# Attention scores on 32 of TensorE's rows, maxima of two batches beside the experts, exponentials of two banks, in a layer of attention and experts

## The chip, the cores and the metric

The kernel runs on one core of a Trainium2 chip. The metric is device time in microseconds (us): the time of one execution. All times below are in us unless they are marked ns. TensorE does matmuls and transposes, VectorE (DVE) and ScalarE (ACT) work on elements and can read the matmul results in PSUM, GpSimd (POOL) works on SBUF and issues the gathers, SyncE (SP) issues the other DMAs. PSUM has eight banks of 512 float32 a partition.

## The reference

With x of 4 x 512 tokens of 512 features, the layer gives x + attention(xn) + experts(xn), with xn the layer norm of x. Attention has 8 heads of 8 features, for each of 4 batches of 512 tokens. The experts: each token takes the two best of 8 experts, and the mean of their rectified outputs.

```python
    scores = jnp.einsum('bhqd,bhkd->bhqk', q, k)
    attn = jax.nn.softmax(scores, axis=-1) / jnp.asarray(HEAD_DIM ** 0.5, x.dtype)
    out = jnp.einsum('bhsl,bhlv->bhsv', attn, v)
...
    logits = x @ W_gate + b_gate
    _, top_idx = jax.lax.top_k(logits, TOP_K)
    y_all = jax.nn.relu(jnp.einsum('bsd,edh->bseh', x, W_e) + b_e)
    y = jnp.take_along_axis(y_all, top_idx[..., None], axis=2)
    return y.mean(axis=2)
```

## The kernel before

The program has no scheduler: each engine's list of work is written out by hand, each engine runs its list in order, and semaphores tie the lists together. A number in parentheses is a line of the kernel.

**Stages.** First come layer norm, projections and routing (to about 107 us). Then 39 expert tiles of 128 gathered token rows (NS is 39). For each tile TensorE turns the next tile's rows with four transposes (1060) and runs twelve matmuls of 512 columns into ps_s (1080); ScalarE copies the turned rows (568) and does the ReLU (573); VectorE makes the low part (798) and adds the expert's bias (830); GpSimd adds half the output bias (475) and gathers later rows (460). Then comes attention: 32 units, eight a batch. A unit is one half of the heads (g, four heads) and 128 keys.

**A head on the array.** The queries and keys of four heads lie in one tile of 128 partitions, 32 a head (q_t, k_t): low and high parts, and in the first rows the negative row maximum against ones, so that a logit comes out of the matmul with its maximum already subtracted. k_head holds, for each head, a copy of the 32 rows of k_t with zeros in the other 96. A matmul over all 128 partitions thus gives one head. The copies are made by DMAs from SyncE (load_heads, 358); k_head is cleared by VectorE (835, 848) and GpSimd (473, 488, 490).

**Scores and maxima.** For the row maxima, scores (988) gives 128 queries against 512 keys of one head, into one bank, and maximum (803) reduces it on VectorE. A batch has 32 of each. The 32 of batch 0 run beside expert tiles, two a tile from tile 21 (SCORES_AT); the other 96 run in the attention units, four a unit, in the first 24 units (unit_scores, with LAG). lay_max (811) writes the finished maxima into the token-wise tile lay, and a fill turns them into q_t.

**Units.** logits (1004) gives 128 keys against 512 queries of one head in ps_t, which has two banks used in turn; ScalarE takes the exponential of one bank (629); values (1015) multiplies the four heads' exponentials with v and ones, 9 columns a head, in ps_o. TensorE's order in a unit is: two logits with a score behind each, the fills of the middle, the values of the unit before, two logits with scores, the fills of the end.

**Fills.** misc_plan (231) names the jobs between: k and q (turning a tile of keys or queries, 972), max, o (976), turn (980), out (984, 985: the output projection, which VectorE adds to the residual, 891). All go through ps_m, whose two banks are used in turn; a fill waits until its bank was read two jobs before. tile_jobs (245) names the fills beside expert tiles.

**Layout and sums.** lay_out (286) splits queries or keys into high and low parts in the tile lay, in one piece for each 128 tokens: by GpSimd for batches 0 and 3, by VectorE for 1 (in expert tiles 33 to 36) and 2 (after the experts). After the experts GpSimd gathers the experts' rows onto the residual in acc, 32 gathers (501), and the layout of q for batch 3 stands at i == 8 among them.

## Time and profile before

| | us |
|---|---|
| runs | 389.19, 388.20, 389.71 |
| median | 389.19 |
| span of the profiled execution | 390.1 |
| TensorE, matmuls, busy | 334.0 (86%) |
| VectorE busy | 260.2 (67%) |
| GpSimd busy | 204.8 (53%) |
| ScalarE busy | 172.6 (44%) |
| mean granted clock of TensorE, as a share of 2.4 GHz | 0.874 |

The profiled execution's own time is the span from its first to its last instruction, 390.1, 0.9 above the median of the runs. Busy TensorE time counts matmuls whose records overlap (a 512-column matmul has a record of 0.39 and starts 0.23 behind the one ahead), so it is read by starts, not by sums. A share of busy time is a mean over stages with different limits; the rows below are therefore taken by stage. "issue" as a releaser is time in which the engine waited for nothing that the profile shows. x8 in a row is eight records; the four values matmuls of a unit are eight records.

### The profile page before, as it was taken

The page shows a single profiled execution, that of the slowest core. Times are in us where ns is not written, and L with a number is a line of the kernel's source. Part 1 is how long each engine was busy: PE and PEld are TensorE (multiplying, and loading weights), DVE is VectorE, ACT ScalarE, POOL GpSimd, SP SyncE. Part 2 cuts the span into 40 slices and gives each one's busy share as a digit, 9 for nine tenths or more (in the row PEclk, how much of TensorE's full clock was granted, in tenths as well). Part 3 has the DMA queues.
Part 4 walks back from the last instruction along what each step waited for, and adds up shares of the span by engine and source line. Part 5 has one row for each costly group of instructions (what it writes and reads, how often), then busy time and mean ns, then how long its engine had stood idle before and what let it go on. Part 6 is the DMA issues. An engine that isn't in the chain of part 4 may idle for free.

```text
span 390.1 us, 5604 instructions
## 1 busy us (share of the span) xinstructions
PE 334.0 (86%) x1629; PEld 238.5 (61%) x1629; DVE 260.2 (67%) x583; ACT 172.6 (44%) x304; POOL 204.8 (53%) x216
## 2 busy tenths in 40 slices
PE   1386888684869999999999998939999999999965
PEld 1265777683848888888888876705455655544412
DVE  4288888857913444466767789597878889785313
ACT  1454444461023333333323322435786777667740
POOL 2155555556474777777665573276688888100000
PEclk9996555556559999999999999977999999999995
DMA  8776765315052545555544441254999999610112
GB/s 232 273 287 221 242 226 188 109 55 216 0 163 83 167 163 164 168 165 186 189 140 146 147 124 54 74 146 97 199 293 241 200 204 148 130 55 0 55 54 108
DMA packets 31004, 59.60 MB, mean 153 GB/s; under 512 B 5504, under 2 KB 5632, under 8 KB 30848
## 3 DMA queue, kind: packets, MB, share of 16 engines
q1 hardware_dynamic: 23248, 40.63, 29.9%
q0 software_dynamic: 7728, 18.62, 22.7%
q8 instruction: 15, 0.25, 0.3%
q14 instruction: 13, 0.11, 0.1%
HBM read 38.52 MB, written 18.61 MB: 146 GB/s over the span
## 4 chain that ended last, share of the span: by engine, by line
PE 67%; DVE 17%; issue 5%; ACT 5%; DMA 3%; SPq 2%; POOL 0%; ACTq 0%; DVEq 0%; POOLq 0%
PE ps_s L1080 28%; PE ps_t L1012 10%; PE ps_o L1027 8%; PE ps_s L1001 6%; PE ps_t L1060 4%; DVE small L678 3%; PE ps_m L972 2%; DVE t_lo L689 2%; DMA stage<-in_L_ffn_W_e_dram 2%; ACT probs L629 2%; DVE stats L661 2%; PE ps_s L946 2%; DVE small L669 2%; DVE hot_row L783 1%; PE ps_m L984 1%
## 5 line engine op out<-in xcount | busy, mean ns | idle before, releaser
L1080 PE MATMUL ps_s<-w_split,t_hi 128*128 x312 | 101.7, 407 | 2.2 <-issue 2.2
L629 ACT ACTIVATE probs<-ps_t 128x512 f32<-128x512 f32 x128 | 69.6, 597 | 34.7 <-PE ps_t L1012 26.7
L809 DVE TENSOR_REDUCE row_max<-ps_s 128x1 f32<-128x512 f32 x112 | 72.2, 684 | 14.2 <-PE ps_s L1001 10.4
L475 POOL TENSOR_TENSOR row_mid<-row_mid,bias_o 128x512 f32<-128x512 f32 x39 | 50.8, 1304 | 47.6 <-ACT row_mid L573 47.6
L573 ACT ACTIVATE row_mid<-row_mid 128x512 f32<-128x512 f32 x39 | 24.7, 632 | 94.6 <-DVE row_mid L830 88.3
L1080 PEld LDWEIGHTS ps_s<-w_split,t_hi 128*128 128x128 f32 x312 | 56.6, 191 | 13.6 <-issue 3.3
L1080 PE MATMUL ps_s<-w_split,t_lo 128*128 x156 | 61.9, 396 | 0.0
L436 POOL TENSOR_TENSOR w_split<-stage,w_split 128x1024 fp32r<-128x1024 f32 x16 | 37.8, 2368 | 45.0 <-ACT w_split L522 45.0
L1012 PE MATMUL ps_t<-q_t,k_head 128*128 128x512 f32 x128 | 57.2, 458 | 3.1 <-ACT probs L629 2.7
L501 POOL DMA_INDIRECT acc<-expert_rows,slots_i x32 | 49.8, 1556 | 12.5 <-issue 8.2
L1012 PEld LDWEIGHTS ps_t<-q_t,k_head 128*128 128x128 f32 x128 | 23.9, 191 | 44.3 <-ACT probs L629 31.0
L830 DVE TENSOR_TENSOR row_mid<-ps_s,bias_e 128x512 f32<-128x512 f32 x39 | 27.0, 692 | 32.0 <-PE ps_s L1080 27.2
L798 DVE TENSOR_TENSOR t_lo<-ps_t,t_hi 128x512 fp32r<-128x512 f32 x39 | 26.9, 691 | 29.1 <-ACT t_hi L568 28.6
L1001 PE MATMUL ps_s<-k_head,q_t 128*128 128x512 f32 x112 | 44.7, 399 | 0.0
L460 POOL DMA_INDIRECT row_in<-xn_rows,gather_i x39 | 38.0, 975 | 11.6 <-DVE gather_i L793 5.4
L1027 PE MATMUL ps_o<-probs,v_ones 128*9 128x512 f32 x256 | 34.3, 608 | 5.9 <-issue 4.9
L1080 PEld LDWEIGHTS ps_s<-w_split,t_lo 128*128 128x128 f32 x156 | 29.7, 190 | 6.8
L932 PE MATMUL ps_t<-ident,row_mid 128*128 128x128 f32 x64 | 17.4, 427 | 15.9 <-ACT row_mid L554 15.9
L946 PE MATMUL ps_s<-wp_hi,t_hi 128*128 128x200 f32 x64 | 26.2, 409 | 4.0 <-issue 1.9
L1060 PE MATMUL ps_t<-ident,row_in 128*128 128x128 f32 x156 | 24.3, 280 | 3.4 <-DMA row_in<-xn_rows,gather_i 3.4
L1060 PEld LDWEIGHTS ps_t<-ident,row_in 128*128 128x128 f32 x156 | 19.7, 143 | 8.9 <-issue 3.7
L946 PE MATMUL ps_s<-wp_lo,t_hi 128*128 128x200 f32 x64 | 24.8, 388 | 0.0
(132 smaller groups left out, 488.4 us busy)
## 6 DMA issues: line engine op xcount, KB each, us to landing
expert_rows<-row_mid SPq DMA_DIRECT2D x39, 256.0 KB, 2.0
stage<-in_L_ffn_W_e_dram SPq DMA_DIRECT2D x16, 512.0 KB, 5.1
row_in<-in_L_attn_x_dram SPq DMA_DIRECT2D x16, 256.0 KB, 4.1
xn_rows<-row_mid SPq DMA_DIRECT2D x16, 256.0 KB, 2.6
acc<-in_L_attn_x_dram SPq DMA_DIRECT2D x16, 256.0 KB, 3.9
out_dram<-res SPq DMA_DIRECT2D x16, 256.0 KB
bias_e<-in_L_ffn_b_e_dram SPq DMA_DIRECT2D x1, 2048.0 KB, 7.2
k_head<-k_t SPq DMA_DIRECT2D x32, 64.0 KB, 2.0
```

The lines of the kernel that those rows point to most:

```text
L436: pool.tensor_tensor(w_split[:, e, 1, cs, :], stage[:, c % RW, :, :], w_split[:, e, 0, cs, :].bitcast(F32), ALU.subtract).then_inc(w_lo_ma ...
L460: pool.indirect_dma_start(row_in[:, n % RI, :], None, xn_dram, bass.IndirectOffsetOnAxis(ap=gather_i[:, n:n + 1], axis=0)).then_inc(rows_i ...
L475: pool.tensor_tensor(row_mid[:, n % 4, :], row_mid[:, n % 4, :], bias_o[:], ALU.add).then_inc(y_done, 1)
L501: pool.indirect_dma_start(acc[:, i, :], None, y_dram, bass.IndirectOffsetOnAxis(ap=slots_i[:, r, i:i + 1], axis=0), compute_op=ALU.add).th ...
L629: act.activation(probs[:, n % 2, j, :], ps_t[:, j % 2, :], ACT.Exp).then_inc(exp_done, 1)
L809: dve.tensor_reduce(row_max[:, b % 2, h, i:i + 1], score_bank(n), AX.X, ALU.max).then_inc(max_done, 1)
L946: mm = pe.matmul(ps_s[:, i % 2, 0:PW], a[:, i % 2, ks], w[:, c, :], start=(n == 0), stop=(n == 3 * KC - 1))
L1001: pe.matmul(score_bank(n), q_t[b % 3][:, h // HG, i * P:(i + 1) * P], k_head[b % 3][:, h, :], start=True, stop=True).then_inc(scores_ready, 1)
L1012: pe.matmul(ps_t[:, n % 2, :], k_head[b % 3][:, g * HG + j, kt * P:(kt + 1) * P], q_t[b % 3][:, g, :], start=True, stop=True).then_inc(log ...
L1027: mm = pe.matmul(ps_o[32 * j:32 * j + VC, :], v_ones[:, QT * b + kt, g * HG + j, :], probs[:, n % 2, j, :], start=(kt == 0), stop=(kt == Q ...
L1060: mm = pe.transpose(ps_t[:, n % 2, c * P:(c + 1) * P], row_in[:, n % RI, c * P:(c + 1) * P], ident[:])
L1080: mm = pe.matmul(ps_s[:, n % 2, :], a[:, n % 2, ks], rhs, start=(k == 0), stop=(k == 3 * KC - 1))
```

## The change

- logits and scores no longer use k_head. A matmul takes the 32 partitions of its head from q_t and k_t. The tile k_head, its clearing and its 32 DMAs go; k_t has three buffers, not two.
- Logits come in pairs: two heads, two banks of ps_l, one semaphore step. ScalarE takes the exponential of both banks in one instruction of 1024 elements. The unit has two such pairs.
- The banks are dealt anew: ps_l four (in the experts stage two of them are ps_y for the experts and two ps_t for the turned rows), ps_s two for scores alone, ps_o one, ps_m one. So a fill now waits until the job just before it was read, and the first logits wait until the last expert tile's bias was added (y_biased).
- Scores of one head half run over the query tile first and the heads next, beginning with the third head (score_place). Batch 0's scores stand in tiles 1 to 16, batch 1's in tiles 21 to 36, two a tile; the 64 of batches 2 and 3 are spread over 36 half units, from the 11th (half_scores), behind the pair of logits.
- lay_out does all 512 tokens in one piece. Batch 1's is in tile 17 on VectorE, its fills behind tiles 18 and 19; q of batch 3 is laid out by GpSimd at i == 4 of its gathers, not 8. The misc_plan is dealt anew: k 2 and q 2 in batch 0's units, q 3 in unit 8.
- SyncE loads all 16 residual tiles in one go.

```diff
-FREE_0, FREE_1 = NT, 2 * NT
-ZERO_AT = FREE_0 + 1
-COPY_AT = ZERO_AT, ZERO_AT + 2
-SCORES_AT = ZERO_AT + 4
-MAX_AT = SCORES_AT + HG * QT // 2 + 1
-LAY_AT = FREE_1 + 1
-K_AT, Q_AT = LAY_AT + QT - 1, LAY_AT + QT
-assert SCORES_AT + H * QT // 2 <= NS and Q_AT < NS - 1
-LAG = 2
+FREE_0 = NT
+SCORES_AT = (1, FREE_0 + 5)
+MAX_AT = {SCORES_AT[b] + (g + 1) * HG * QT // 2: (b, g) for b in range(2) for g in range(G)}
+LAY_AT = FREE_0 + 1
+K_AT, Q_AT = LAY_AT + 1, LAY_AT + 2
+assert Q_AT < SCORES_AT[1] and SCORES_AT[1] + H * QT // 2 < NS
+LAG, SPREAD = 11, 36
...
 
             plan = {0: ([], []),
-                    1: ([("o", b - 1, 1)], [("max", 0, 1)] if b == 0 else []),
-                    2: ([("k", b + 2, 0)], [("max", b, 1)] if b >= 1 else []),
-                    3: ([("turn", b - 1, 0)], [("k", b + 2, 1)]),
-                    4: ([("out", b - 1, 0)], [("out", b - 1, 1)]),
+                    1: ([("o", b - 1, 1)], [("max", 1, 1)] if b == 0 else []),
+                    2: ([("k", 2, 0)] if b == 0 else [("k", b + 2, 0)], [("k", 2, 1)] if b == 0 else [("max", b, 1)] if b >= 2 else []),
+                    3: ([("turn", b - 1, 0)], [("k", b + 2, 1)] if b >= 1 else []),
+                    4: ([("q", 2, 0)] if b == 0 else [("out", b - 1, 0)], [("q", 2, 1)] if b == 0 else [("out", b - 1, 1)]),
                     5: ([("o", b, 0)], [("out", b - 1, 2)]),
-                    6: ([("out", b - 1, 3)], [("max", b + 1, 0)]),
-                    7: ([("q", b + 2, 0)], [("q", b + 2, 1)])}[u]
+                    6: ([("out", b - 1, 3)], [("max", b + 1, 0)] if b >= 1 else []),
+                    7: ([], [])}[u]
+            if b == 1:
+                plan = {0: ([("q", 3, 0)], [("q", 3, 1)])}.get(u, plan)
             return [[j for j in half if 0 <= j[1] < B] for half in plan]
...
-            return {MAX_AT: [("max", 0, 0)], K_AT: [("k", 1, 0), ("k", 1, 1)], Q_AT: [("q", 1, 0), ("q", 1, 1)]}.get(n, [])
+            if n in MAX_AT:
+                return [("max",) + MAX_AT[n]] if MAX_AT[n] != (1, 1) else []
+            return {K_AT: [("k", 1, 0), ("k", 1, 1)], Q_AT: [("q", 1, 0), ("q", 1, 1)]}.get(n, [])
 
         def tile_scores(n):
 
-            return range(2 * (n - SCORES_AT), 2 * (n - SCORES_AT) + 2) if 0 <= n - SCORES_AT < H * QT // 2 else ()
+            for b in range(2):
+                if 0 <= n - SCORES_AT[b] < H * QT // 2:
+                    first = H * QT * b + 2 * (n - SCORES_AT[b])
+                    return range(first, first + 2)
...
+        def score_place(n):
+
+            b, left = divmod(n, H * QT)
+            g, left = divmod(left, HG * QT)
+            i, j = divmod(left, HG)
+            return b, g, (j + 2) % HG, i
+
+        def half_scores(b, u, half):
+
+            n = 2 * (2 * HG * b + u) + half - LAG
+            left = H * QT * (B - 2)
+            return [H * QT * 2 + s for s in range(left * n // SPREAD, left * (n + 1) // SPREAD) if 0 <= s < left]
...
+        def lay_out(eng, step, steps, b, which):
...
-            for i in tiles:
-                for at in hi_at:
-                    eng.tensor_copy(heads[:, i, :, at:at + HE].bitcast(F32R), exact[:, i]).then_inc(step, 1)
-                eng.memset(heads[:, i, :, 0:2], first).then_inc(step, 1)
-                steps[0] += 3
+            for at in hi_at:
+                eng.tensor_copy(heads[:, :, :, at:at + HE].bitcast(F32R), exact).then_inc(step, 1)
+            eng.memset(heads[:, :, :, 0:2], first).then_inc(step, 1)
+            steps[0] += 3
             eng.wait_ge(step, steps[0])
-            for i in tiles:
-                eng.tensor_tensor(heads[:, i, :, lo_at:lo_at + HE], exact[:, i], heads[:, i, :, hi_at[0]:hi_at[0] + HE],
-                                  ALU.subtract).then_inc(laid, 1)
+            eng.tensor_tensor(heads[:, :, :, lo_at:lo_at + HE], exact, heads[:, :, :, hi_at[0]:hi_at[0] + HE],
+                              ALU.subtract).then_inc(laid, 1)
...
-            def load_heads(b, g):
-
-                wait_kept(sp, ("k", b, g))
...
-                for j in range(HG):
-                    rows = slice(32 * j, 32 * j + 32)
-                    sp.dma_start(k_head[b % 3][rows, g * HG + j, :].bitcast(F32), k_t[b % 2][rows, g, :].bitcast(F32)).then_inc(heads_in[b % 3][g], 16)
...
             sp.wait_ge(y_made, NS)
-            for i in range(QT):
+            for i in range(NT):
                 load_acc(i)
-            for g in range(G):
-                load_heads(2, g)
-            for i in range(QT, NT):
-                load_acc(i)
-            for g in range(G):
-                load_heads(3, g)
...
-                if n == NS - 1:
-
-                    pool.wait_ge(y_biased, NS)
-                    pool.memset(k_head1[:, 2:4, :].bitcast(F32), 0.0).then_inc(heads_zero[1], 1)
...
-                if n == FREE_1 - 1:
-
-                    pool.wait_ge(y_made, FREE_1)
+                if n == FREE_0 - 1:
+
+                    pool.wait_ge(y_made, FREE_0)
                     pool.memset(lay_2[:], 0.0).then_inc(lay_zero, 1)
                     pool.memset(lay_1[:], 0.0).then_inc(lay_zero, 1)
...
-            pool.wait_ge(y_made, NS)
-            pool.wait_ge(y_biased, NS)
-            for hs in (slice(4, 6), slice(6, 8)):
-                pool.memset(k_head1[:, hs, :].bitcast(F32), 0.0).then_inc(heads_zero[1], 1)
-            for h in range(0, H, 2):
-                pool.memset(k_head2[:, h:h + 2, :].bitcast(F32), 0.0).then_inc(heads_zero[2], 1)
...
-                if i == NT // 2:
+                if i == QT:
...
+                    for pair in range(2):
+                        act.wait_ge(logits_ready, 2 * n + pair + 1)
+                        if pair == 0 and n >= 2:
 
                             act.wait_ge(pv_done, n - 1)
-                        act.activation(probs[:, n % 2, j, :], ps_t[:, j % 2, :], ACT.Exp).then_inc(exp_done, 1)
-                        if j == 1:
+                        act.activation(probs[:, n % 2, 2 * pair:2 * pair + 2, :], ps_l[:, 2 * pair:2 * pair + 2, :],
+                                       ACT.Exp).then_inc(exp_done, 1)
...
-                dve.tensor_reduce(row_max[:, b % 2, h, i:i + 1], score_bank(n), AX.X, ALU.max).then_inc(max_done, 1)
+                dve.tensor_reduce(row_max[:, b % 2, HG * g + j, i:i + 1], ps_s[:, n % 2, :], AX.X, ALU.max).then_inc(max_done, 1)
+                if (n + 1) % (HG * QT) == 0:
+                    lay_max(b, g)
...
-                if m >= 2:
-
-                    pe.wait_ge(misc_freed[m % 2], m // 2)
-                bank = ps_m[:, m % 2, :]
+                if m == 0:
+
+                    pe.wait_ge(weights_split, 6)
+                else:
+                    pe.wait_ge(misc_freed, m)
+                bank = ps_m[:]
...
+            def scores(n):
+
+                b, g, j, i = score_place(n)
+                if n % (HG * QT) == 0:
+                    wait_kept(pe, ("k", b, g))
+                    wait_kept(pe, ("q", b, g))
+                if n < 2:
+
+                    pe.wait_ge(gather_ready, 1)
+                else:
+                    pe.wait_ge(max_done, n - 1)
+                rows = slice(32 * j, 32 * j + 32)
+                pe.matmul(ps_s[:, n % 2, :], q_t[b % 3][rows, g, i * P:(i + 1) * P], k_t[b % 3][rows, g, :],
                           start=True, stop=True).then_inc(scores_ready, 1)
...
+                n = 2 * (2 * HG * b + u) + pair
                 if n >= 2:
                     pe.wait_ge(exp_done, n - 1)
...
-                pe.matmul(ps_t[:, n % 2, :], k_head[b % 3][:, g * HG + j, kt * P:(kt + 1) * P], q_t[b % 3][:, g, :],
-                          start=True, stop=True).then_inc(logits_ready, 1)
+                for j in (2 * pair, 2 * pair + 1):
+                    rows = slice(32 * j, 32 * j + 32)
+                    mm = pe.matmul(ps_l[:, j, :], k_t[b % 3][rows, g, kt * P:(kt + 1) * P], q_t[b % 3][rows, g, :],
+                                   start=True, stop=True)
+                mm.then_inc(logits_ready, 1)
...
             pe.wait_ge(rows_lo, NS)
+            pe.wait_ge(y_biased, NS)
...
+                    for half, jobs in enumerate(misc_plan(b, u)):
+                        logits(b, u, half)
+                        for n in half_scores(b, u, half):
+                            scores(n)
                         for job in jobs:
                             fill(*job)
```

What the order of the lists becomes. In TensorE's list, at the tile whose fills turn the keys of batch 1 (before tile 36, in the change tile 18), before (t_hi, t_lo: the tile's rows; lay_2: keys of batch 1):

```order
L1080 MATMUL ps_s<-w_split,t_hi 128x512
L1080 MATMUL ps_s<-w_split,t_lo 128x512
L1001 MATMUL ps_s<-k_head0,q_t0 128x512 [waits max_done]
L1001 MATMUL ps_o<-k_head0,q_t0 128x512 [waits max_done]
L972 MATMUL ps_m<-ident,lay_2 128x128 [waits k_laid1,misc_freed1]
L972 MATMUL ps_m<-ident,lay_2 128x128 x3
L972 MATMUL ps_m<-ident,lay_2 128x128 [waits k_laid1,misc_freed0]
L972 MATMUL ps_m<-ident,lay_2 128x128 x3
L1068 TENSOR_LOAD expert_i
```

and in the change, where ps_l is also the experts' bank:

```order
L1031 MATMUL ps_l<-w_split,t_lo 128x512
L924 MATMUL ps_m<-ident,lay_2 128x128 [waits k_laid1,misc_freed]
L924 MATMUL ps_m<-ident,lay_2 128x128 x3
L924 MATMUL ps_m<-ident,lay_2 128x128 [waits k_laid1,misc_freed]
L924 MATMUL ps_m<-ident,lay_2 128x128 x3
L1019 TENSOR_LOAD expert_i
```

The two scores are gone from this tile, and the second fill now waits for misc_freed, the copy of the first. In TensorE's list, one unit of attention with scores, before:

```order
L1012 MATMUL ps_t<-q_t0,k_head0 128x512 [waits exp_done]
L1001 MATMUL ps_s<-k_head1,q_t1 128x512 [waits max_done]
L1012 MATMUL ps_t<-q_t0,k_head0 128x512 [waits exp_done]
L1001 MATMUL ps_s<-k_head1,q_t1 128x512 [waits max_done]
L1012 MATMUL ps_t<-q_t0,k_head0 128x512 [waits exp_done]
L1001 MATMUL ps_s<-k_head1,q_t1 128x512 [waits max_done,misc_freed0,heads_in1_1]
L1012 MATMUL ps_t<-q_t0,k_head0 128x512 [waits exp_done]
L1001 MATMUL ps_s<-k_head1,q_t1 128x512 [waits max_done]
L1027 MATMUL ps_o<-probs,v_ones 9x512 [waits v_laid,exp_done]
L1027 MATMUL ps_o<-probs,v_ones 9x512 x3
```

and in the change (L965 logits, L952 scores, L932 a fill, L978 values):

```order
L965 MATMUL ps_l<-q_t1,k_t1 128x512 [waits exp_done]
L965 MATMUL ps_l<-q_t1,k_t1 128x512
L952 MATMUL ps_s<-k_t2,q_t2 128x512 [waits max_done] x2
L965 MATMUL ps_l<-q_t1,k_t1 128x512 [waits exp_done]
L965 MATMUL ps_l<-q_t1,k_t1 128x512
L952 MATMUL ps_s<-k_t2,q_t2 128x512 [waits max_done] x2
L932 MATMUL ps_m<-ident,o_tok 128x128 [waits o_laid,misc_freed]
L932 MATMUL ps_m<-ident,o_tok 128x128 x3
L978 MATMUL ps_o<-probs,v_ones 9x512 [waits v_laid,exp_done]
L978 MATMUL ps_o<-probs,v_ones 9x512 x3
```

Four waits of logits have become two, a score no longer stands between two logits, and the fill stands between the scores and the values. In VectorE's list, the tile with the layout of batch 1, before (one of four such tiles; lay_2 keys, lay_1 queries):

```order
L830 TENSOR_TENSOR row_mid<-ps_s,bias_e 128x512
L809 TENSOR_REDUCE row_max<-ps_s 128x1 [waits scores_ready]
L809 TENSOR_REDUCE row_max<-ps_o 128x1 [waits scores_ready]
L294 CAST lay_2<-proj 128x8x8 [waits lay_zero]
L294 CAST lay_2<-proj 128x8x8
L295 MEMSET lay_2 128x8x2
L299 TENSOR_TENSOR lay_2<-proj,lay_2 128x8x8 [waits dve_step]
L294 CAST lay_1<-proj 128x8x8 x2
L295 MEMSET lay_1 128x8x2
L299 TENSOR_TENSOR lay_1<-proj,lay_1 128x8x8 [waits dve_step]
L798 TENSOR_TENSOR t_lo<-ps_t,t_hi 128x512 [waits rows_hi]
```

and in the change, with the row maxima of batch 0 laid ahead of it:

```order
L770 TENSOR_REDUCE row_max<-ps_s 128x1 [waits scores_ready] x2
L780 TENSOR_SCALAR lay_0<-row_max 128x4x4 [waits q_laid0,max_done]
L781 SCALAR_TENSOR_TENSOR lay_0<-row_max,lay_0 128x4x4 [waits dve_step]
L294 CAST lay_2<-proj 128x32x8 [waits lay_zero]
L294 CAST lay_2<-proj 128x32x8
L295 MEMSET lay_2 128x32x2
L298 TENSOR_TENSOR lay_2<-proj,lay_2 128x32x8 [waits dve_step]
L294 CAST lay_1<-proj 128x32x8 x2
L295 MEMSET lay_1 128x32x2
L298 TENSOR_TENSOR lay_1<-proj,lay_1 128x32x8 [waits dve_step]
L759 TENSOR_TENSOR t_lo<-ps_l,t_hi 128x512 [waits rows_hi]
```

The pieces of four tiles stand in one, ahead of the low part (L759) for which the next tile's matmuls wait.

## Rows read from the trace of the kernel before

**Rows 1.** Busy time by stretch: busy us (instructions) per engine, granted clock, DMA

```profile
300.00:320.00 20.00, 20.00 (x114) 11.75 (x112) 16.85 (x34) 14.11 (x28) 17.34 (x26) 1.00 1.00 209
...
360.00:380.00 20.00, 16.23 (x83) 5.90 (x82) 4.90 (x17) 11.94 (x23) 0.00 (x0) 1.00 0.14 53
```

**Rows 2.** Chain that ended last, expert tiles 1, 2 and 38: start, us, what

```profile
119.17 2.76 PE ps_s L1080 x12
122.36 2.77 PE ps_s L1080 x12
...
249.69 2.76 PE ps_s L1080 x12
```

**Rows 3.** Timeline, TensorE, end of tile 30: start, us, engine, line, what

```profile
218.52 0.39 PE L1080 MATMUL ps_s<-w_split,t_lo 128*128 x1
218.75 0.39 PE L1001 MATMUL ps_s<-k_head,q_t 128*128 128x512 f32 x1
218.97 0.39 PE L1001 MATMUL ps_o<-k_head,q_t 128*128 128x512 f32 x1
219.21 0.60 PE L972 MATMUL ps_m<-ident,lay 128*128 128x128 f32 x4
219.64 0.60 PE L1060 MATMUL ps_t<-ident,row_in 128*128 128x128 f32 x4
```

**Rows 4.** Timeline, TensorE, the first values

```profile
261.60 1.90 PE L1027 MATMUL ps_o<-probs,v_ones 128*9 128x512 f32 x8 [4.94 <-issue]
```

**Rows 5.** Timeline, ScalarE, the first exponentials

```profile
253.84 3.44 ACT L629 ACTIVATE probs<-ps_t 128x512 f32<-128x512 f32 x6
```

**Rows 6.** Timeline, VectorE, in the hole

```profile
254.38 6.54 DVE L817 TENSOR_SCALAR lay<-row_max 128x16 fp32r<-128x16 f32 x1
```

**Rows 7.** Timeline, GpSimd, in the hole

```profile
257.24 3.64 POOL L490 MEMSET k_head<- 128x1024 f32 x4
```

**Rows 8.** Timelines, last unit: TensorE, then ScalarE

```profile
373.82 1.04 PE L1027 MATMUL ps_o<-probs,v_ones 128*9 128x512 f32 x8
374.80 0.73 PE L1012 MATMUL ps_t<-q_t,k_head 128*128 128x512 f32 x2
...
375.33 1.08 ACT L629 ACTIVATE probs<-ps_t 128x512 f32<-128x512 f32 x2 [0.81 <-PE ps_t L1012]
```

**Rows 9.** Timeline, TensorE, a unit with scores

```profile
304.39 0.39 PE L985 MATMUL ps_m<-wo_lo,o_t 128*128 128x512 f32 x1
304.71 1.05 PE L1027 MATMUL ps_o<-probs,v_ones 128*9 128x512 f32 x8
305.69 0.50 PE L1012 MATMUL ps_t<-q_t,k_head 128*128 128x512 f32 x1
306.02 0.39 PE L1001 MATMUL ps_s<-k_head,q_t 128*128 128x512 f32 x1
```

**Rows 10.** Timelines, tail: TensorE, then VectorE

```profile
382.56 0.77 PE L984 MATMUL ps_m<-wo_hi,o_t 128*128 128x512 f32 x1 [0.78 <-ACT o_t L598]
383.12 0.63 PE L985 MATMUL ps_m<-wo_lo,o_t 128*128 128x512 f32 x1
...
386.85 0.69 DVE L891 TENSOR_TENSOR res<-ps_m,acc 128x512 f32<-128x512 f32 x1 [0.17 <-PE ps_m L985]
```

**Rows 11.** Timeline, ScalarE, behind tile 36

```profile
246.24 0.63 ACT L573 ACTIVATE row_mid<-row_mid 128x512 f32<-128x512 f32 x1 [3.43 <-DVE row_mid L830]
246.77 1.06 ACT L598 ACTIVATE k_t<-ps_m 128x512 fp32r<-128x512 f32 x2
```

**Rows 12.** Groups by line: busy us, mean ns, idle before; ScalarE, 1024 elements

```profile
L522 ACT ACTIVATE w_split<-stage 128x1024 fp32r<-128x1024 f32 x16 | 16.7, 1044 | 3.9 <-DMA stage<-in_L_ffn_W_e_dram 3.9
```

**Rows 13.** Timeline, VectorE, two maxima

```profile
306.45 1.29 DVE L809 TENSOR_REDUCE row_max<-ps_s 128x1 f32<-128x512 f32 x2 [0.67 <-PE ps_s L1001]
```

**Rows 14.** Timeline, GpSimd, gathers onto the residual

```profile
284.50 1.55 POOL L501 DMA_INDIRECT acc<-expert_rows,slots_i  x1 [0.30 <-issue]
286.36 1.55 POOL L501 DMA_INDIRECT acc<-expert_rows,slots_i  x1 [0.31 <-issue]
```

153 lines of the change are left out of this document (46 added, 107 removed).

## The prediction

> **What bounds the kernel now.** I read the busy time by stretch first. In the middle of the attention stage TensorE is busy for the whole stretch, 20.00 of 20 us, at granted clock 1.00, with VectorE at 16.85 and ScalarE at 14.11 [rows 1]. So there TensorE sets the pace, VectorE is next, and ScalarE has room. The chain that ended last names the experts' matmuls one tile after the other: tile 1 starts at 119.17, tile 2 at 122.36, tile 38 at 249.69 [rows 2]. A tile without extra work thus takes 3.20, and 37 of them would take 118.4; the stage took 130.5, so scores, fills and layout cost 12.1 on the path. The timeline of TensorE shows what they are made of: two score matmuls take the places from 218.75 to 219.21, 0.23 each, and a fill of four transposes 0.43 [rows 3]. Sixteen tiles with two scores are 7.4, five fills about 2.2, and the rest, 2.5, is VectorE's layout of batch 1 in four tiles. Then comes a hole: the first values start at 261.60 [rows 4], although ScalarE began the exponentials at 253.84 [rows 5]. One small VectorE instruction, due at 254.38, took 6.54 us [rows 6]; GpSimd was clearing padded key copies in that time [rows 7]. From 261.60 to the values of the last unit, about 376.5 (the exponentials at 375.33 end at 376.41 [rows 8]), 31 units take 114.9, 3.71 each. The tail is 13.6.
>
> **The experts stage after the change.** It must now hold 32 tiles with two scores instead of 16. The second score of a tile uses other rows of the array and another bank. No row shows such a pair. Above it is bounded by two full matmuls, 0.46, plus leaving and entering a narrower use of the array. The values, which use 9 columns each, show that price: they start 0.32 after the matmul ahead instead of 0.23, and the first full matmul behind them holds its place for 0.33 [rows 9], so about 0.1 on each side. Below it is bounded by one matmul and no price, 0.23. I take 0.23 for the first, 0.11 for the second (the place that one transposed block takes, 0.43 for four [rows 3], in which its weights are loaded) and 0.2 for the two sides: 0.54 a tile, 17.3 in all (7.4 to 21.1 at the bounds).
> Beside it stand seven fills at 0.43, 3.0. Two tiles have two fills each, and ps_m is now one bank: the second fill waits until ScalarE has copied the first, which in its queue comes behind the tile's ReLU, which waits for VectorE's bias. From the start of the tile's last matmul that is 0.39 to its end [rows 3], 0.69 for the bias (as long as the sum at 386.85 [rows 10]), 0.63 and 0.60 on ScalarE [rows 11] and 0.1 of signals, 2.4, where before the second fill started after 0.66. That is 1.75 twice, 3.5. The layout of batch 1 is one piece of VectorE work in one tile now, without TensorE work to spare in the next; it cost 2.5 before in four tiles. With a quarter of the instructions I take 1.3 (0 to 2.7). Sum 25.1 against 12.1: **13.0 lost**.
> The Trainium skill, TensorEngine Tiling (Array Packing), Key Properties, says that changing the tiling mode drains the engine. It speaks against putting scores between full matmuls; the 0.1 on each side above is what the trace shows of it for columns, and no row here shows it for rows.
>
> **The hole.** The clearing on GpSimd and on VectorE goes, and with it the wait of the copy DMAs. The new wait for the last tile's bias ahead of the first logits holds TensorE about 0.7, behind which stand only logits. From 254.0 two exponentials of two banks take 2.0 (one of 1024 elements a row takes 1.044 [rows 12]), so the first values start near 256.0: **5.6 won**. What was hidden by that hole, the copies of v and the layout of batch 2, is short and needed only in unit 1 and later.
>
> **The attention stage.** Scores fall from 96 in 24 units to 64 in 18 units, and logits come in pairs. In a unit without scores the chain is values, second pair of logits, exponential of two banks, values. Values to logits is 0.98 [rows 9]. The first logits start at 374.80 and the exponential at 375.33 [rows 8], so 0.53, and the second of the pair comes 0.11 later; then 1.04 and 0.1: 2.76. Thirteen such periods and three copies of sums at 0.6 that lie in the chain: 37.7.
> In the 18 units with scores VectorE is next. A maximum takes a place of 0.60 (two in 1.29 [rows 13]). The other VectorE work is about 0.9 a unit, by the stretch of 20 us in which there were no maxima and 5.5 units, 4.90 busy [rows 1]. 64 maxima in 18 units are 2.13 a unit, so VectorE alone asks for 3.0. But TensorE runs in order: a score waits for the maximum two before it, and the values stand behind the scores. From a unit's second score: 0.1, a fill in three units of four with its entering and leaving, 0.4, values 0.98, logits and the next score 0.2, its latency 0.5, two maxima 1.2: 3.4. Eight of 36 half units have one score, which takes 0.3 off; results and head sums that don't fit a gap put 0.2 on: 3.3 (3.0 to 3.8). 18 such periods are 59.4. Together 97.1 against 114.9: **17.8 won**.
> GpSimd's layout of q for batch 3 now stands behind 8 gathers, 1.86 from one to the next [rows 14]. With a first gather 8 after the experts it is done about 25 after them, and TensorE asks for it at 1 + 6 x 2.76 + 2 x 3.3 + 0.4, 24.6. No cover is left there; I put 0, and up to 3 in the range.
>
> **The tail.** The last four results shared two banks and took 4.98, from 382.56 to 387.54 [rows 10]. With one bank each must be read before the next is filled: the pair of matmuls at the low clock 1.19 (382.56 to 383.75), the sum 0.69, signals 0.1, 2.0 for each: **3.0 lost**. Nothing changes ahead of the experts: the fills there have over a microsecond to spare.
>
> **The sum.** 390.1 + 13.0 - 5.6 - 17.8 + 3.0 = 382.7 of span. The median of the runs is 389.19, 0.9 below the profiled span, so I take 0.9 off: 381.8.
>
> **The rivals.**
> - Rows one after another (slower). If matmuls on different rows don't overlap, a pair costs 0.46 + 0.2 in a tile: 21.1, so 16.8 lost there. In the attention stage a half unit's block of four takes 0.92 instead of 0.56: 3.75 with scores, 2.9 without, 107 in all, 7.9 won. 390.1 + 16.8 - 5.6 - 7.9 + 3.0 = 396.4, so 395.5. For it: every row of this trace with full arrays shows 0.23 for each. Against it: the eight records of a unit's values, 512 columns each, take 0.98 together [rows 9], 0.12 each, which they can only do side by side. It decides once the second of a pair costs more than about 0.17.
> - Full overlap. The second costs nothing and VectorE alone paces the scored units: 0.43 a tile, 9.4 lost; 3.1 and 2.65 a unit, 92, 22.9 won: 374.0, so 373.1.
> - A wash. The order on TensorE couples it to VectorE more than I think, say 3.7 a scored unit, 7.2 more: 389.0. For it: PE's queue has a fill ahead of the values in most units.
> - The clock falls. With a busy share of three quarters TensorE could be granted 1.2 GHz. After the hole of 4.9 us the values took 1.90 instead of 0.98 [rows 4]. Each unit would be 1.2 to 1.4 longer, 40 in all: 422. Against it: with 16.23 of 20 busy the clock was 1.00 [rows 1].
>
> On overlap, the Trainium skill, TensorE: Matmul & The Clock Gate, Part 3, gives a speedup of 3.07 for four matmuls on 32 rows each. As an estimate from that page a block of four would take 0.30 instead of my 0.56, which is the full-overlap rival; no row of this case shows it.
>
> **How the numbers follow.** Forecast 0.45, full overlap 0.20, rows one after another 0.20, wash 0.10, clock 0.05. The forecast's own spread, from the bounds of the pair and of the period, is 377 to 388. The range runs from the full overlap to the serial rows, 373 to 396. A measurement of this kernel tells about 0.5%, 387.2 to 391.1, from no change. Faster gets all of full overlap and nearly all of the forecast, 0.65; slower gets the serial rows and the clock, 0.23; the rest, 0.12, is within.
>
> **What would show it.** Tiles with scores should be 3.74 apart, the tiles with two fills 1.7 longer than their neighbours, values of the first unit within 4 us of the last tile's end, units without scores 2.8 and with scores 3.3 apart with VectorE the busiest there, and the last results 2 apart. The prediction is wrong if the second score of a tile starts a full 0.23 behind the first, if the clock shows 0.5 inside the attention stage, or if TensorE waits for maxima or for the layout of q much longer than this.

## The result, and the profile after

The changed kernel is slower. Its runs took 400.39, 401.69, 403.96 and 411.15, median 402.82, against 389.45 for the kernel before on the same chip: ratio 1.033, 95% interval 1.028 to 1.037. The forecast was 381.8, the range 373 to 396. The profiled execution was the longest of the four, span 409.4; a second profile of the same kernel (the first experiment below) has 400.0, and both are used.

The page of the kernel after (the engines' busy times, then two groups of instructions: line, engine, operation, count | busy us, mean ns | idle time before them and what ended it):

```profile
PE 337.1 (82%) x1629; PEld 214.5 (52%) x1629; DVE 247.8 (61%) x530; ACT 167.3 (41%) x240; POOL 189.6 (46%) x161
...
L770 DVE TENSOR_REDUCE row_max<-ps_s 128x1 f32<-128x512 f32 x128 | 82.4, 683 | 23.0 <-PE ps_s L952 23.0
...
L589 ACT ACTIVATE probs<-ps_l 128x1024 f32<-128x1024 f32 x64 | 63.7, 1024 | 37.8 <-PE ps_l L965 37.1
```

VectorE's maxima waited 23.0 in all for TensorE's scores, and ScalarE's exponentials 37.1 for its logits, while TensorE was busy 82% of the span. So I read by stage, from the starts in TensorE's timeline:

| stage | before | after, 409.4 | after, 400.0 | forecast of the change |
|---|---|---|---|---|
| start of tile 1 | 118.9 | 119.3 | 119.4 | 0 |
| tile 1 to the end of the last tile's matmuls | 133.5 | 148.6 | 148.6 | +13.0 |
| from there to the first values | 9.2 | 3.5 | 3.5 | -5.6 |
| first values to the last unit's | 114.9 | 120.7 | 110.2 | -17.8 |
| from there to the end | 13.6 | 17.4 | 18.4 | +3.0 |

The hole came out as forecast. Experts lost 15.1 instead of 13.0, and the tail 3.8 and 4.8 instead of 3.0. Attention is where the forecast failed.

**Experts.** Timeline of TensorE in the kernel after, from tile 1 into tile 2 (start, us, what, count), the counterpart of [rows 3]:

```profile
121.86 0.39 PE L1031 MATMUL ps_l<-w_split,t_lo 128*128 x1
122.18 0.50 PE L952 MATMUL ps_s<-k_t,q_t 32*128 32x512 f32 x2
122.61 0.66 PE L1011 MATMUL ps_l<-ident,row_in 128*128 128x128 f32 x4
123.03 0.70 PE L1031 MATMUL ps_l<-w_split,t_hi 128*128 x2
```

The two scores together take 0.50, as long as one record of such a matmul in [rows 9]: they do lie side by side. But the first starts 0.32 behind the matmul ahead, where a full one started 0.23 behind it [rows 3], and the transposes start 0.43 later. Tiles with a pair are 3.76 apart, tiles without 3.20: 0.56 a pair, forecast 0.54.

The stall on the single fill bank, in the chain of the kernel after, tile 18 (the keys of batch 1):

```profile
188.60 0.70 DVE row_mid L793
...
189.32 0.63 ACT row_mid L534
189.96 0.49 ACT k_t L558
...
190.49 0.66 PE ps_m L924 x4
```

The second fill waits for bias, ReLU and copy in turn. The two tiles with two fills take 6.17 and 6.18, and the tile with the layout 5.54.

**Attention, the clock.** Busy time by stretch in the kernel after (length, then TensorE, weight loads, VectorE, ScalarE, GpSimd, granted clock, DMA share, GB/s):

```profile
304.00:308.00 4.00, 3.12 (x21) 1.20 (x20) 2.82 (x5) 2.53 (x3) 3.29 (x3) 1.00 0.94 143
308.00:312.00 4.00, 4.00 (x20) 1.64 (x19) 1.58 (x3) 1.82 (x3) 3.39 (x3) 0.58 0.95 142
312.00:316.00 4.00, 4.00 (x15) 1.00 (x15) 1.43 (x3) 1.46 (x3) 3.39 (x3) 0.50 0.90 139
...
348.00:352.00 4.00, 4.00 (x15) 1.95 (x12) 2.29 (x4) 2.39 (x3) 0.00 (x0) 0.50 0.17 66
```

TensorE had waits in the first of these stretches (3.12 busy of 4), and then it worked at 1.2 GHz, and so it did again from 346 to 367. Four units that lie wholly or nearly so in these stretches take 5.9 to 6.4, where the other profile has 3.8 to 4.4. In the kernel before the granted clock was 1.00 in the middle of attention [rows 1]. These stretches are the 10.5 us by which attention is longer in this profile than in the other.

**The tail.** VectorE's last results in the kernel after, the counterpart of [rows 10]; each waits for the pair of matmuls that waited for the result before:

```profile
401.64 0.69 DVE L846 TENSOR_TENSOR res<-ps_m,acc 128x512 f32<-128x512 f32 x1 [1.41 <-PE ps_m L937]
403.74 0.69 DVE L846 TENSOR_TENSOR res<-ps_m,acc 128x512 f32<-128x512 f32 x1 [1.41 <-PE ps_m L937]
405.84 0.69 DVE L846 TENSOR_TENSOR res<-ps_m,acc 128x512 f32<-128x512 f32 x1 [1.41 <-PE ps_m L937]
```

They are 2.10 apart, forecast 2.0.

### The profile page after: what moved, and what is told of

It is laid out like the page before. It is cut to its first block, busy times and chain, and to the rows that moved or that the text cites. A ratio compares the mean times of both kernels' runs of the same rounds, so it can differ in the third digit from the quotient of the medians.

```text
span 409.4 us, 5391 instructions
## 1 busy us (share of the span) xinstructions
PE 337.1 (82%) x1629; PEld 214.5 (52%) x1629; DVE 247.8 (61%) x530; ACT 167.3 (41%) x240; POOL 189.6 (46%) x161
## 4 chain that ended last, share of the span: by engine, by line
PE 62%; DVE 21%; ACT 7%; issue 4%; DMA 3%; SPq 2%; DVEq 0%; ACTq 0%; POOLq 0%
PE ps_l L1031 27%; PE ps_o L978 9%; PE ps_s L952 6%; PE ps_l L1011 5%; PE ps_l L965 5%; DVE small L639 3%; ACT probs L589 3%; DVE row_max L770 3%; PE ps_m L924 2%; PE ps_m L936 2%; DVE t_lo L650 2%; DMA stage<-in_L_ffn_W_e_dram 2%; DVE stats L622 2%; PE ps_s L896 2%; DVE small L630 2%
## 5 line engine op out<-in xcount | busy, mean ns | idle before, releaser
L1031 PE MATMUL ps_l<-w_split,t_hi 128*128 x312 | 100.9, 404 | 1.7 <-issue 1.3
L589 ACT ACTIVATE probs<-ps_l 128x1024 f32<-128x1024 f32 x64 | 63.7, 1024 | 37.8 <-PE ps_l L965 37.1
L1031 PEld LDWEIGHTS ps_l<-w_split,t_hi 128*128 128x128 f32 x312 | 56.4, 191 | 12.6 <-issue 2.8
L1031 PE MATMUL ps_l<-w_split,t_lo 128*128 x156 | 61.5, 394 | 0.0
L793 DVE TENSOR_TENSOR row_mid<-ps_l,bias_e 128x512 f32<-128x512 f32 x39 | 27.0, 691 | 44.6 <-PE ps_l L1031 44.6
L952 PE MATMUL ps_s<-k_t,q_t 32*128 32x512 f32 x128 | 40.5, 504 | 6.5 <-DVE row_max L770 6.0
L432 POOL DMA_INDIRECT row_in<-xn_rows,gather_i x39 | 38.0, 975 | 16.9 <-DVE gather_i L754 10.5
L978 PE MATMUL ps_o<-probs,v_ones 128*9 128x512 f32 x256 | 40.4, 708 | 5.7 <-ACT probs L589 5.5
L759 DVE TENSOR_TENSOR t_lo<-ps_l,t_hi 128x512 fp32r<-128x512 f32 x39 | 26.9, 691 | 18.4 <-ACT t_hi L529 18.4
L965 PEld LDWEIGHTS ps_l<-q_t,k_t 32*128 32x128 f32 x128 | 11.5, 204 | 41.5 <-issue 21.8
L1031 PEld LDWEIGHTS ps_l<-w_split,t_lo 128*128 128x128 f32 x156 | 29.5, 189 | 6.6
L965 PE MATMUL ps_l<-q_t,k_t 32*128 32x512 f32 x128 | 30.3, 552 | 2.0 <-ACT probs L589 1.1
L882 PE MATMUL ps_l<-ident,row_mid 128*128 128x128 f32 x64 | 17.4, 428 | 15.4 <-ACT row_mid L515 15.4
L952 PEld LDWEIGHTS ps_s<-k_t,q_t 32*128 32x128 f32 x128 | 16.6, 200 | 23.8 <-issue 12.7
L1011 PE MATMUL ps_l<-ident,row_in 128*128 128x128 f32 x156 | 26.2, 292 | 2.6 <-DMA row_in<-xn_rows,gather_i 2.2
```

Of the source, the lines that this page charges most:

```text
L432: pool.indirect_dma_start(row_in[:, n % RI, :], None, xn_dram, bass.IndirectOffsetOnAxis(ap=gather_i[:, n:n + 1], axis=0)).then_inc(rows_i ...
L589: act.activation(probs[:, n % 2, 2 * pair:2 * pair + 2, :], ps_l[:, 2 * pair:2 * pair + 2, :], ACT.Exp).then_inc(exp_done, 1)
L952: pe.matmul(ps_s[:, n % 2, :], q_t[b % 3][rows, g, i * P:(i + 1) * P], k_t[b % 3][rows, g, :], start=True, stop=True).then_inc(scores_read ...
L965: mm = pe.matmul(ps_l[:, j, :], k_t[b % 3][rows, g, kt * P:(kt + 1) * P], q_t[b % 3][rows, g, :], start=True, stop=True)
L978: mm = pe.matmul(ps_o[32 * j:32 * j + VC, :], v_ones[:, QT * b + kt, g * HG + j, :], probs[:, n % 2, j, :], start=(kt == 0), stop=(kt == Q ...
L1011: mm = pe.transpose(ps_t[:, n % 2, c * P:(c + 1) * P], row_in[:, n % RI, c * P:(c + 1) * P], ident[:])
```

## Experiments: why attention gave so little

**After again.** No edit.

> The changed kernel itself, unaltered, for a second profile beside the first one, in which TensorE's granted clock fell to 0.50 in two stretches of attention (308 to 322 and 348 to 366 us). Theory A (the clock falls because TensorE works in attention at about 0.8 of the time only, with gaps): stretches at 0.50 are there again, though perhaps at other places or one fewer; time 400 to 405. Theory B (the two stretches were an accident of that one execution): granted clock 1.00 from 285 us to the end, and about 16 us less span than 409.4, so about 393, and the same excess of the median is then spread over the units and the experts stage.

Measured: median 404.17 of 6 runs (397.18 to 414.14), span 400.0. This is theory A's total, and its slow stretches are there, but shorter: at the start of attention (0.75 from 270 to 275, then 0.57 to 280) and from 320 to 325 at 0.66. Attention takes 110.2. So the clock is the smaller part of the miss in this profile: at nearly full clock the stage won 4.7, not 17.8. Timeline of TensorE in this run, a period without scores, from values to values:

```profile
369.13 1.04 PE L978 MATMUL ps_o<-probs,v_ones 128*9 128x512 f32 x8 [0.45 <-ACT probs L589]
370.10 0.50 PE L965 MATMUL ps_l<-q_t,k_t 32*128 32x512 f32 x2
370.54 0.51 PE L936 MATMUL ps_m<-wo_hi,o_t 128*128 128x512 f32 x1
370.88 0.39 PE L937 MATMUL ps_m<-wo_lo,o_t 128*128 128x512 f32 x1
371.20 0.50 PE L965 MATMUL ps_l<-q_t,k_t 32*128 32x512 f32 x2
372.15 0.66 PE L928 MATMUL ps_m<-ident,o_sum 128*128 128x128 f32 x4 [0.46 <-DVE res L846]
372.74 1.05 PE L978 MATMUL ps_o<-probs,v_ones 128*9 128x512 f32 x8
```

This period has two fills and takes 3.61; those with one or none take 2.6 to 2.7. With scores, periods with at most one fill take 2.9 to 3.5, about the 3.3 of the forecast, but for two of 4.1 and 4.2, and one of 4.2 at the slow clock; those with two fills take 3.7 to 4.4, and 4.7 at the slow clock.

**All rows.** In scores and logits: `rows = slice(0, P)`, and the exponential's input scaled by 0.001. Each matmul then sums four heads.

> After, but every score and every logit matmul takes all 128 rows instead of one head's 32, with the exponential's input scaled down so that values stay finite. It computes the sum over four heads in place of one head, so its output is not the reference's; order, waits, banks and sizes are after's. Theory A (use of 32 rows makes TensorE's activity low, and the clock falls in attention): granted clock 1.00 throughout attention, no unit of about 6 us; a unit costs more columns of work (scores and logits one after another, up to 3.9 us against 3.3), experts' score pairs 0.10 cheaper each (3 us over 32 tiles); total 385 to 397, below after's 402.8. Rival R (the clock has nothing to do with it; order, the two-bank exponentials and VectorE's maxima make the time): total above after, 410 or more, since the same order now has 31 x about 0.8 us more of TensorE work.

Measured: 401.06 (399.34 to 402.65), ratio 1.032. Both totals were wrong. The clock is 1.00 from 267 us to the last unit, as theory A said; attention takes 113.0, since scores and logits no longer overlap. In the experts a pair costs 0.45 (tiles 3.65 apart). So in after's order 32 rows win about what they cost. Beside its wider matmuls this kernel has other values and a busier TensorE; the experiments on short maxima and on one row group below bear on these two.

**Warm matmuls in all of attention.** Ahead of each logits pair:

```
+    for j in (2 * pair, 2 * pair + 1):
+        pe.matmul(ps_l[:, j, :], k_t[...][:, g, kt * P:(kt + 1) * P], q_t[...][:, g, :], start=True, stop=True)
```

> After, with two more full-array matmuls (all 128 rows, 512 columns) into the same banks ahead of each logits pair in attention; the real logits overwrite them, so the output is unchanged. It adds 128 matmuls of about 0.25 us, 32 us of TensorE work, of which the gaps (about 0.6 us per unit, 20 us in all) can hide a part. Theory A (low activity drops the clock): no stretch at 0.50 after 285 us, units 3.3 to 3.7 us throughout, total 385 to 400, no longer than after. Rival R (the clock falls for another reason, or activity is not what counts): stretches at 0.50 stay and the total rises by 12 to 32 us, to 415 to 435.

Measured: 419.67 (417.55 to 422.47), ratio 1.081. No stretch of attention is below 1.00, but a unit without scores or a fill takes 3.26 instead of 2.60 and one with scores mostly 4.0 or more: the added work lies in the chain. The clock half of theory A holds, the price half doesn't.

**Short maxima.** `ps_s[:, n % 2, 0:32]` for batches 2 and 3, and the exponential's input scaled by 0.001. The maxima leave out 480 of 512 keys.

> After, with the maxima of batches 2 and 3 (those taken in attention) read from 32 of 512 keys only, and the exponential's input scaled down so that values stay finite: the maxima are not the reference's, so its output is not either. VectorE's maximum costs about 0.1 instead of 0.68 us. Theory A' (TensorE's waits of 0.6 to 0.8 us for VectorE's maxima make the gaps that lower its activity, and then the clock falls): units with scores 2.7 us instead of 3.3, clock 1.00 in attention, total 402.8 less 18 x 0.6 less 9 to 16 us of slow clock, 377 to 384. Rival (the clock falls because only 32 rows are used, whether there are gaps or not): stretches at 0.50 remain, total 390 to 397.

Measured: 392.52 (390.32 to 392.95), in the rival's range. Attention 102.5; scored units with at most one fill mostly 2.6 to 2.9, as theory A' said, but those with two still 3.7 to 3.9, and the clock was 0.50 from 270 to 275 and 0.79 to 0.86 from 290 to 300. Waiting for maxima costs about 0.7 in units with one fill and up to 0.5 in those with two; and without it the clock still fell.

**One row group for all heads.** `rows = slice(0, 32)` in scores and logits, and the exponential's input scaled by 0.01. All heads of a half then use the first one's rows.

> After, but all heads use the same 32 rows (0 to 31) for scores and logits, with the exponential's input scaled down; the output is not the reference's. The matmuls stay 32 rows wide but can no longer lie side by side, so TensorE is as busy as with 128 rows (0.9 or more of the time in attention), and narrow. Theory W (the width of the matmuls is what lets the clock fall): stretches at 0.50 in attention remain, total 402 or more, above the 128-row kernel's 401. Theory B (only the busy share counts): clock 1.00 throughout attention as with 128 rows, total 400 to 403, attention 113.

Measured: 462.11 (453.86 to 480.5), ratio 1.187. Theory W, and far beyond it. Stretches of this run, and under them the same time in the run with all rows:

```profile
295.00:300.00 5.00, 4.91 (x28) 2.32 (x21) 3.36 (x11) 2.44 (x4) 4.39 (x6) 1.00 1.13 219
300.00:305.00 5.00, 4.80 (x19) 2.35 (x18) 3.07 (x5) 2.75 (x4) 4.46 (x6) 0.79 0.75 101
305.00:310.00 5.00, 5.00 (x18) 1.99 (x16) 1.29 (x2) 2.24 (x4) 4.08 (x4) 0.50 0.93 133
```

```profile
295.00:300.00 5.00, 4.71 (x32) 2.27 (x31) 4.76 (x14) 3.35 (x4) 4.11 (x3) 1.00 0.88 119
300.00:305.00 5.00, 4.81 (x26) 2.46 (x23) 2.59 (x5) 2.54 (x3) 4.37 (x3) 1.00 0.95 150
305.00:310.00 5.00, 5.00 (x27) 2.87 (x26) 3.26 (x5) 3.85 (x5) 4.08 (x4) 1.00 0.94 143
```

TensorE is as busy in both, and only the narrow one falls to 0.50; it stays at 0.50 from 355 to 420 us. Where its clock is 1.00, at the end of attention, its units take the same 2.82 as with all rows, so the clock makes the difference. What I had put the fall down to in the rival, a TensorE that is less busy, isn't needed for it: with as much to do, the narrow matmuls lost the clock and the full ones kept it. That narrow matmuls always lose it isn't shown, and kernels below kept it with them. In the experts of this run tiles with a pair are 4.00 apart, 0.80 a pair.

**A free bank in the last eight units.** On the two-bank kernel below, the fills of batch 3's units alternate too (`n_late` is their first), and their second bank is one of the scores':

```
+        side = [0 if n_pre <= m < n_late else m % 2 for m in range(len(misc))]
+            return ps_m[:] if side[m] == 0 else ps_o[:] if m < n_pre else ps_s[:, 0]
```

> After with two fill banks outside attention, and also in batch 3's units (the last eight), where one of the score banks is free. There the three units with a second fill took 3.67, 3.62 and 3.69, those without 2.59. Theory S (the second fill's 1.05 us comes from waiting for the single bank to be read): these units go to 2.7 to 3.0, 2.0 to 3.0 us less in all, total 389 to 390. Rival (they are long because two fills of 0.6 stand on TensorE between values and logits): 3.4 or more, less than 0.8 us less in all, 391 to 392.

Measured: 391.86 (389.89 to 404.85). The same place as above, now with the two fills in different banks:

```profile
363.86 1.05 PE L991 MATMUL ps_o<-probs,v_ones 128*9 128x512 f32 x8 [0.33 <-ACT probs L600]
364.83 0.50 PE L978 MATMUL ps_l<-q_t,k_t 32*128 32x512 f32 x2
365.26 0.50 PE L949 MATMUL ps_m<-wo_hi,o_t 128*128 128x512 f32 x1
365.60 0.40 PE L950 MATMUL ps_m<-wo_lo,o_t 128*128 128x512 f32 x1
365.93 0.50 PE L978 MATMUL ps_l<-q_t,k_t 32*128 32x512 f32 x2
366.36 0.66 PE L941 MATMUL ps_s<-ident,o_sum 128*128 128x128 f32 x4
366.95 1.05 PE L991 MATMUL ps_o<-probs,v_ones 128*9 128x512 f32 x8
```

The 0.46 of waiting is gone and the unit takes 3.09; the three such units take 3.01, 3.09 and 3.16. Of the 1.05 that a second fill cost, 0.57 was the bank and about 0.5 its place on TensorE. Each theory has half. The total shows no difference from the kernel that it is built on; in this profile the clock also fell twice later in attention (0.67 from 335 to 340, 0.70 from 350 to 355).

## Experiments: the parts of the change

**Two banks outside attention.** After, with a second fill bank in the values' bank beside the experts and in a logit bank in the tail.

```
+    side = [0 if n_pre <= m < n_att else m % 2 for m in range(len(misc))]
+    turn_no = [side[:m].count(side[m]) for m in range(len(misc))]
+    def misc_bank(m):
+        return ps_m[:] if side[m] == 0 else ps_o[:] if m < n_pre else ps_l[:, 0]
```

> After, with a second fill bank beside the experts (the values' bank, unused there) and in the tail (a logit bank, unused there); attention as in after. Theory: the two tiles with two fills take 4.1 instead of 6.4 and 6.2, 4.3 less; the last four results 1.2 apart instead of 2.1, 3.4 less; attention unchanged at 110; span 400.0 less 7.7, so 392, total 391 to 396. Rival (the stalls in those tiles are the layout's, not the bank's): experts unchanged, total 397 to 400.

Measured: 391.91 (390.17 to 404.64), ratio 1.005, interval 1.001 to 1.009, as the theory said. The two tiles with two fills take 4.07 and 4.08, 4.2 less; the last values to the end 14.3 instead of 18.4; attention 108.6. One bank outside attention thus cost about 8 of the 13 us by which after is slower.

**Batch 1 back in attention.** On that kernel: `SCORES_AT = (1,)`, `LAG, SPREAD = 4, 48`; the fills of batch 1's and 2's maxima move along.

> As the kernel with two fill banks outside attention, and with batch 1's 32 scores and maxima moved back out of the experts into attention (96 scores in 24 units, 4 each, instead of 64 in 18). Theory: experts lose 16 pairs of 0.56, 9.0 us; attention gets 6 more scored units, at 0.7 each 4.2, and 0.3 for the fuller ones, in all 4 to 9: total 387 to 394, 0 to 5 us below the kernel it is built on. Rival (TensorE's coupling to VectorE grows with 4 scores a unit and the clock dips more): attention 14 us or more above, total 396 or more.

Measured: 393.1 (389.10 to 396.06), profiled span 389.1. Tile 1 to the first values takes 138.1 instead of 147.9, attention 118.5 instead of 108.6. What leaves the experts comes back in attention, part of it through the clock, which was between 0.66 and 0.85 in five stretches of 5 us from 290 to 345: no difference that these runs can tell.

**Exponentials one bank at a time.** After with `ps_t[:, j % 2, :]` for the logits and `m % 2` for all fills.

> After, with exponentials one bank at a time again, and the two banks that this frees given to the fills: two fill banks everywhere (beside the experts the second is the bank of the values, which is unused there). Theory S (in attention the single fill bank costs what the paired exponentials win: the units with a second fill take 3.6 to 3.7 without scores and 4.2 with, against 2.6 and 3.3): unscored units without fills 2.9 instead of 2.6, units with fills 0.5 to 0.8 shorter, attention 104 to 110 against 110.2; with experts 4.3 and tail 3.4 shorter, total 388 to 393. Rival (the order of fills and values is what costs, not the bank): attention 112 to 116, total 395 to 399.

Measured: 419.06 (411.47 to 430.12), profiled span 428.3, ratio 1.072, against both theories. More than half of attention ran at 0.50 (units of 5.6 to 6.3), and in the rest a unit without scores took 3.07. With that clock the run doesn't settle the question of banks; the free bank above does. It does show the pairs' worth in one place: at full clock the unit without scores and fills took 3.07 here and 2.59 in the second profile of after.

**The rows alone in the kernel before.** `rows = slice(32 * j, 32 * j + 32)` on k_t in scores and logits; copies, clearing and their DMAs gone, a third buffer for k_t; order, banks and exponentials as before.

> The kernel before with one part of the change alone: scores and logits read one head's 32 rows of k_t and q_t, and the padded key copies, their clearing and their DMAs are gone. Staging, order, two fill banks and single-bank exponentials stay as before. Theory (the copies cost the hole of 5 to 6 us and nothing else; rows cost about 0.1 per score pair in a tile and save nothing where two matmuls behind each other use the same rows; TensorE is 100% busy in attention, so the clock holds): first values 5 us earlier, 16 tiles 0.1 longer, attention 114 to 117, total 384 to 387. Rival (32-row matmuls by themselves cost the time in attention, by mode changes or by the clock): attention over 119, total 392 or more.

Measured: 391.05 (386.88 to 392.51), ratio 1.002, interval 0.998 to 1.006: above the theory's 387, below the rival's 392. First values 3.4 earlier; attention 116.6, of which the first four units, at a clock of 0.50, take 20.5. A pair in a tile costs 0.80 (tiles 4.00 apart): both scores of a tile belong to one head. Timeline of TensorE:

```profile
224.55 0.50 PE L953 MATMUL ps_s<-k_t,q_t 32*128 32x512 f32 x1
224.88 0.39 PE L953 MATMUL ps_o<-k_t,q_t 32*128 32x512 f32 x1
225.21 0.66 PE L1013 MATMUL ps_t<-ident,row_in 128*128 128x128 f32 x4
```

The second starts 0.33 behind the first, where a full one started 0.22 behind [rows 3].

**The same with all rows.** `rows = slice(0, P)` in that kernel, again with the exponential's input scaled by 0.001 and sums over four heads.

> The kernel before with the 32-row scores and logits alone, but each of these matmuls widened to all 128 rows, exponential's input scaled down so that values stay finite. It computes sums over four heads, so its output is not the reference's; order, waits and the hole are those of the 32-row kernel. Theory A (the width of the matmuls decides how the clock comes back after the hole): after at most one unit at 0.50 the clock is 1.00, as in the kernel before; second to fourth unit 3.1 to 3.9 instead of 4.9, 5.2 and 4.5; total 384 to 387. Rival (width does not matter, the hole does): the same four slow units, total 390 to 392.

Measured: 382.83 (382.37 to 383.78), ratio 0.983, 8 us below the same kernel with 32 rows. Stretches at the hole, first with 32 rows, then with all:

```profile
255.00:260.00 5.00, 3.66 (x14) 1.13 (x14) 4.66 (x24) 3.76 (x7) 1.38 (x1) 0.86 0.41 136
260.00:265.00 5.00, 5.00 (x22) 2.38 (x20) 2.94 (x20) 3.33 (x6) 3.15 (x17) 0.50 0.99 326
265.00:270.00 5.00, 4.74 (x24) 1.41 (x16) 2.67 (x4) 2.17 (x4) 4.39 (x3) 0.50 1.05 380
```

```profile
250.00:255.00 5.00, 3.21 (x11) 1.68 (x9) 3.23 (x9) 3.03 (x6) 2.15 (x2) 1.00 0.14 52
255.00:260.00 5.00, 4.99 (x32) 2.31 (x31) 4.89 (x35) 4.12 (x8) 2.25 (x14) 1.00 0.94 284
260.00:265.00 5.00, 5.00 (x29) 2.67 (x26) 3.72 (x7) 3.15 (x7) 4.24 (x6) 1.00 1.02 373
265.00:270.00 5.00, 4.92 (x30) 2.54 (x32) 4.11 (x7) 4.35 (x9) 2.29 (x2) 1.00 1.08 278
```

The hole is as long in both, 4.1, and only the narrow kernel loses the clock. Theory A, and a total below its 384: attention is 4.4 shorter, the experts 3.5 (a pair costs 0.45 instead of 0.80) and the tail 1.8.

**Full matmuls in the hole.** Three kernels with added matmuls of 128 rows into the values' bank ahead of the first values:

```
+    for _ in range(count):
+        pe.matmul(ps_o[:], wo_hi[:, 0:P], wo_hi[:], start=True, stop=True)
```

> The kernel before with the 32-row scores and logits alone (no padded copies), plus eight full 128-row matmuls of 512 columns into the values' bank in the wait ahead of the first values, whose results are overwritten. Without them that kernel ran its first four attention units at granted clock 0.50, from 260 to 275 us, and they took 20.5 us. Theory A (the clock falls in the hole and TensorE with 32-row matmuls does not bring it back for four units): the clock stays 1.00, these four units take 13.5 to 15, total 391.1 less 5 to 7, so 383 to 386, below the kernel before. Rival (the fall has its cause in the 32-row work of those units, not in the hole): units still at 0.50, total 390 to 392.

> The kernel before, unchanged but for 26 full matmuls into the values' bank in the 5 us hole ahead of the first values (overwritten). Question: how much of the gain of the 32-row kernel with such matmuls (386.6 against 390.0) is the matmuls' own. Theory 1 (the clock at 0.50 after the hole costs the first unit of before 6.37 instead of 3.8): 2 to 3 us won, 387 to 388, so that the 32-row part by itself brings only about 1 us. Theory 2 (before returns to full clock soon enough): 0 to 1 won, 389 to 390.

> After with the second fill bank outside attention, plus nine full 128-row matmuls in the wait between the last tile and the first values, into the values' bank (overwritten). Theory A: the clock holds 1.00 through the first units, the first two take 3.7 and 3.7 instead of 4.6 and 3.8, total 391.9 less 1 to 2, 389.5 to 391, so level with the kernel before. Rival: the clock falls anyway, 391 to 393.

Measured: the 32-row kernel 386.62 (384.93 to 388.34), ratio 0.993 (0.990 to 0.995), clock 1.00 throughout attention, as theory A said. The kernel before, with 26 such matmuls, 388.69, ratio 0.996 (0.995 to 0.998), between its two theories: its first two units take 8.1 instead of 9.7. After with two banks, with nine, 401.14 (395.37 to 402.86), 9 us worse than without: its first three units took 3.67, 2.60 and 2.60, better than theory A said, but then, still narrow and with waits, TensorE was granted 0.58 to 0.74 in four of the five stretches of 5 us from 290 to 315, and the total was above the rival's 393 too. Here, holding the clock at one place only moved its fall. The profile, with a span of 393.6, shows only a part of that loss.

> The same, and eleven more such full matmuls in the waits of the tail, behind the last values (3, then 6, then 2). Now the tail runs at granted clock 0.50 and takes 14.8 us from the last values to the end. Theory A: clock 1.00 through the fills and results of the tail, each fill 0.4 and each result pair 0.4 shorter, 1.5 to 2.5 us less than the kernel without them: 381 to 384. Rival (the added matmuls lie in the chain, or the clock falls all the same): 0 to 2 us more than the kernel without them.

Measured: 386.07 (383.26 to 386.16). From the last values to the end 14.1 instead of 14.8, a gain of 0.7 where theory A said 1.5 to 2.5, and the clock was 0.50 from 370 to 375 all the same; the runs overlap with those of the kernel without these matmuls.

**Row groups apart.** The 32-row kernel in the order of before, with after's order of heads, so that neighbouring scores use different row groups: `return HG * g + (j + 2) % HG, i`; with and without the added full matmuls.

> The kernel before with 32-row scores and logits and the added full matmuls in the hole and in the tail (386.1), in which neighbouring scores now belong to different heads, in after's order, so that they use different row groups. Theory P (a score pair costs a tile 0.80 on one row group, 4.00 against 3.20, and 0.56 on two, 3.76 against 3.20, as in after): 16 tiles 0.24 shorter, 3.8 us less in the experts stage; in attention logits and scores overlap more, 0 to 2 less; total 380 to 383. Rival C (the more they overlap, the less busy TensorE is, and the clock falls in attention for 5 us or more): stretches at 0.50, total 386 or more.

> The same without any of the added full matmuls, so the kernel before with after's 32 rows and after's order of heads and nothing else. Theory P: experts 3.8 us shorter than in the first 32-row version (391.1), but the first four units at 0.50 again after the hole: 386 to 388. Rival C: the clock falls in further stretches of attention, 390 or more.

Measured: 382.94 (381.94 to 384.00), ratio 0.982 (0.979 to 0.985), and without added matmuls 383.37 (382.77 to 384.29), ratio 0.984 (0.981 to 0.987). The first is theory P. The second is below theory P's 386, which had expected four slow units. The page and the timeline of the one without:

```profile
PE 323.5 (85%) x1629; PEld 214.0 (56%) x1629; DVE 248.8 (65%) x578; ACT 171.5 (45%) x304; POOL 199.0 (52%) x209
```

```profile
226.99 0.50 PE L962 MATMUL ps_s<-k_t,q_t 32*128 32x512 f32 x1
227.00 0.50 PE L962 MATMUL ps_o<-k_t,q_t 32*128 32x512 f32 x1
227.42 0.66 PE L1022 MATMUL ps_t<-ident,row_in 128*128 128x128 f32 x4
```

Both scores start together, the tiles are 3.76 apart, attention takes 109.7 against 114.9 before, and the clock is 1.00 from 265 us to the last unit; only the first unit is slow, 4.78. In the profile with the added matmuls the clock fell once, to 0.50 from 355 to 360, which is rival C in small: it cost 2.4, of about 3.6 that they had won in the hole and in the tail. Both versions beat before and after. So of the whole change, the 32 rows with their order of heads win 6 us, and the rest (banks, pairs of exponentials, layout in one piece, the maxima of batch 1 beside the experts), put on top of them, loses 19, the lower clock included.

What wins these 6 us is for the most part that the padded copies can go, not the narrow matmuls. The kernel without copies and with all rows, which computes sums over four heads, had 382.83. Against it the narrow one wins 2.5 in attention (109.7 against 112.2) and loses 1.0 in the experts and 1.8 in the tail, where its clock is at 0.50 from 366 instead of from 372. The hole is 4.1 in both, and 9.2 in the kernel before.

## Why the prediction was wrong, point by point

In the second profile the span is 17.3 above the forecast 382.7. Attention has 13.1 of it, the experts 2.1, the tail 1.8, the rest is 0.3.

- **Experts, +13.0; measured +15.1.** Pairs 0.56 (0.54 said). Double fills 4.2 (3.5 said), shown by giving them a second bank. The layout in one piece makes its tile 2.3 longer than a plain one, where I said 1.3.
- **Hole, -5.6; measured -5.7.** Right, and for the reason given.
- **Attention, -17.8; measured -4.7 at nearly full clock, +5.8 in the first profile.** The failed step: the length of a unit. I charged one fill in three scored units of four, and no unit with a second fill or with a wait for the single bank; 12 of the 31 periods have two fills. I gave scored units 3.3 and the others 2.90 on average (2.76, and three copies of 0.6 among the 13). In the two-bank kernel, whose attention is after's and which had only its first two units slow, 18 scored units took 66.7 (3.71 each) and 13 others 41.9 (of it 2.1 for the slow clock, 4.61 and 3.80 against 3.67 and 2.60 in the run that kept it), against 59.4 and 37.7. That is 9.4 at full clock; the other 3.7 of the 13.1 are the clock in the second profile. The base periods are near what I said (3.4 for scored units with at most one fill, 2.6 for the others against 2.76); a second fill adds about 1 (0.7 with scores), because the single bank must be read first (0.57) and because it stands on TensorE between logits and values. The wait on the bank is shown by the free bank, in three units without scores; for those with scores it is taken to be the same. Of the bank I had charged the experts' stalls and the tail's, and not attention's. The size is the wash rival's 3.7 a scored unit, which I gave 0.10; it named the fill ahead of the values, but as a coupling to VectorE.
- **The clock.** The forecast had no term for it. I gave the rival 0.05 and a price of 40 us, for the whole stage; 0.5 inside attention was my own sign of being wrong, and it showed. It came in stretches, and after's runs reach from 397 to 414 where before's reach from 387 to 392. My argument against it was that before held 1.00 with 16.23 of 20 busy [rows 1], but those were matmuls of 128 rows. On 32 rows of one group the clock was 0.50 with TensorE busy throughout, and with all rows in the same order 1.00. No row of before had a matmul on 32 rows, and I took width for harmless because no row spoke of it.
- **Tail, +3.0; measured +3.8 and +4.8.** Results 2.10 apart (2.0 said); the second bank gives 4.1 back.
- **Layout of q for batch 3, 0.** Right: no unit near it is longer than its fills make it.
- **Full overlap and rows one after another.** Two matmuls on different groups start together, as full overlap says; but beyond its columns a pair costs 0.33 more (0.56 less the 0.23 of one matmul; 0.80 less 0.46 on one group), which I put down to going in and out of the narrow form. I had said 0.2 for that and 0.11 for the second score, which costs 0.01: two errors that cancel, so that 0.54 was near by luck. The Trainium skill, TensorEngine Tiling (Array Packing), Key Properties, says that changing the tiling mode drains TensorE. The runs agree that there is a price, up to this 0.33 for in and out; they don't show a drain as its cause.

**Open.** Which mixture of narrow matmuls and waits brings the clock down isn't settled. Narrow on one group fell under full load in after's order. In the order of before, with logits going round the groups, three kernels had full matmuls added in the hole: one held 1.00 throughout attention, and two had one late fall each. Without them the clock was 0.50 for 17 us with both scores of a tile on one group, and for 3 us with the groups apart. In after's order, which has more waits, it fell too. Scaled exponentials aren't what kept the clock in the kernels with all rows: two kernels with 32 rows and scaled exponentials (short maxima, one row group) lost it. Whether the paired exponentials are a gain in total wasn't isolated: the run meant for it was overrun by the clock, and shows only the 0.48 above, for one unit.

## What to carry to other kernels

Look for what a narrow form lets you leave out: here most of its gain was the padded copies. For the matmuls themselves, let neighbours lie on different row groups (383.37 against 391.05 here, the better clock included), and don't put them in small numbers between full ones, where each time in and out cost 0.33. Look at the granted clock as soon as part of TensorE's work becomes narrow, before any other reading. When banks are dealt anew, go through every place where two jobs follow each other on the bank that became single, in all stages.

## What the hardware showed that I had not expected

- A pair of scores between full matmuls costs a tile 0.45 at 128 rows, 0.56 on two groups of 32 rows, and 0.80 on one group (3.65, 3.76 and 4.00 against 3.20 between tiles). On one group the second starts 0.33 behind the first; full ones were 0.22 apart. That gap goes with the change of form: of four logits in a row on one group the second started 0.34 behind the first and the next two 0.23 behind the one ahead, and four at 128 rows behind the values, which use 9 columns, did the same (0.34, 0.24, 0.23).
- TensorE at 32 rows on one group was granted 1.2 GHz from 355 to 420 us while it was busy for 64.5 of these 65. At 128 rows, in the same order and as busy (14.5 of 15 us against 14.7), it had 2.4 GHz.
- After the wait ahead of attention the 32-row kernel needed four units to come back to 2.4 GHz, and the same kernel with 128 rows kept it. The kernel before, whose wait was 5 us longer, lost it too, from 258 to 268.
